# Differences of the feed-forward weights: GpSimd's subtraction, or a DMA that adds the weight onto the negated mean

## The chip, the cores and the metric

One core of a Trainium2 chip runs the kernel. The metric is the device time of one launch in microseconds (us), over several runs.

## The reference, cut to what matters

Two blocks run one after the other on x of 2 x 512 rows and 1024 columns. The first is attention with a small gated layer (256 wide, 1024 inner); its details do not matter here. The second is a feed-forward layer (1024 wide, 3584 inner) whose three weights are first replaced by a coarse form of themselves:

```
def _binary_diff_weight(w, base):
    d = w - base
    coeff = jnp.mean(jnp.abs(d))
    return base + coeff * jnp.sign(d)
W1, W2, W3 = (_binary_diff_weight(w, mean_w) for the three)
gate = jnp.einsum('bsh,ih->bsi', hidden_states, W1)
up = jnp.einsum('bsh,ih->bsi', hidden_states, W3)
h = jax.nn.silu(gate) * up
return jnp.einsum('bsi,hi->bsh', h, W2)
```

`coeff` is one number for a whole weight of 3584 x 1024, so all of `w - base` must have been summed before the first product with that weight is finished. Each weight and its mean are 14.7 MB.

## The kernel before, in words

All is float32. Every product of the feed-forward layer is made in three passes: each operand is split in an upper part (rounded to the matmul's float32r) and a lower part (what is left).

The inner 3584 is cut in 28 tiles j of 128, so each weight has 28 tiles of 128 x 1024 (512 KB). `NEED` lists the 84 of them in the order of use, numbered n: w1, w3, w1, w3 of two tiles j, then (one group later) w2, w2 of the two tiles before. So n = 0 to 7 are w1 and w3 of tiles 0 to 3, n = 8 and 9 the first two of w2. TensorE spends 48 matmuls of 512 columns on each n (lines 1012 and 1034).

A tile is **prepared** in a chain over four engines, in one of three slots `raws[n % 3]` (a weight buffer `raw_w` and a mean buffer `raw_base`): SyncE (SP, line 796 and 797) loads both as soon as the lower part of tile n - 3, which had the slot, is made; GpSimd subtracts the mean (`difference`, line 1735); ScalarE takes the sign (`sign`, L1230); VectorE makes coeff * sign + mean (`whole_weight`, L1533); ScalarE rounds it (`upper`, L1248); VectorE takes the rest (`lower`, L1542).

A tile is **measured** for its coefficient by a load of its own, a subtraction (GpSimd L1730 or VectorE L1700), and a sum of absolute values (ScalarE, `sum_up`, L1225). 70 of the 84 tiles are measured beside the attention block, in an order that a planner writes out. The last 14, all of w2 (t = 70 to 83), are measured at the start of the feed-forward layer in three buffers `late`: SP loads three of them behind the load of each tile n = 5, 6, 7, 8 and the last two behind n = 9 (`LOADED_AFTER`; load t waits for `sum_up` of t - 3), GpSimd subtracts two behind each of its differences n = 5 to 9 (`DIFFERED_AFTER`), VectorE the other four, and ScalarE sums 1, 2, 3, 3, 3, 2 of them at the end of its steps n = 0 to 5 (`SUMMED_IN`).

Behind the planner's part each engine works through n = 0 to 83 in an order that is fixed in the code. ScalarE at step n: round tile n + 2; if n is a w1, silu of the gate of both batches, each of which waits for its products; the sign of tile n + 3 (between the two silus); then the `sum_up`s. TensorE makes the last sum of the coefficient of w2 itself, between steps n = 6 and 7 (L1123): it waits there for VectorE's `csum` (L1521), and that for all 84 tiles. Tiles n = 0, 1, 2 (`EARLY`) are prepared and their first batch is multiplied in the planner's part.

Of the kernel before, what the change touches and what calls it, by code (L numbers as in the profile page):

```python
# [11 lines left out]
ALU = mybir.AluOpType  # L12
ACT = mybir.ActivationFunctionType
# [152 lines left out]
EARLY = len(EARLY_BANK)  # L166
# [194 lines left out]
def phase_one_order():  # L361
# [66 lines left out]
    while ready:  # L428
# [85 lines left out]
NEED = [(which, g - back + kk) for g in range(0, JT + GROUP, GROUP) for kk, which, back in  # L514
        ((0, "w1", 0), (0, "w3", 0), (1, "w1", 0), (1, "w3", 0), (0, "w2", GROUP), (1, "w2", GROUP)) if 0 <= g - back < JT]
# [1 line left out]

LOADED_AFTER, SUMMED_IN = {5: 3, 6: 3, 7: 3, 8: 3, 9: 2}, {0: 1, 1: 2, 2: 3, 3: 3, 4: 3, 5: 2}
SUMMED, LATE_HERE = 6, {1: 2, 2: 5, 3: 8, 4: 11}
DIFFERED_AFTER = {5: 2, 6: 2, 7: 2, 8: 2, 9: 2}  # L520
RAWS, W13, W2 = 3, 3, 3


def bass_layer(nc: bass.Bass, d: dict, out: bass.AP):
    with ExitStack() as whole:
        def sem(name):
            return whole.enter_context(nc.semaphore(name))

        def sems(names):
            return [sem(n) for n in names.split()]  # L530
# [141 lines left out]
        bk_v, fi_v, fi_q, fi_x, fi_var, fi_pow, fi_ok = sems("bk_v fi_v fi_q fi_x fi_var fi_pow fi_ok")  # L672
        me_dve, me_pool, me_abs, c_ones, c_sum, c_mm, c_ok = sems("me_dve me_pool me_abs c_ones c_sum c_mm c_ok")
        n_wk, n_t, n_hi, n_lo = sems("n_wk n_t n_hi n_lo")
        f_diff, f_sign, f_w, f_hi, f_lo = sems("f_diff f_sign f_w f_hi f_lo")
        g_mm, g_silu, g_mul, g_hhi, g_hlo, o_mm, o_acc = sems("g_mm g_silu g_mul g_hhi g_hlo o_mm o_acc")

        order, banks_of, had, turned_had, set_of, set_had, had_last = phase_one_order()
# [112 lines left out]
        @block.sync  # L791
        def _(sp):
            def load_raw(n):
                which, j = NEED[n]
                w, base = raws[n % RAWS]
                sp.dma_start(w[:, :], d[which][j]).then_inc(ld_raw[n % RAWS], 16)
                sp.dma_start(base[:, :], d["mean_" + which][j]).then_inc(ld_raw[n % RAWS], 16)

            sp.dma_start(ident[:, :], d["ident"]).then_inc(ld_const, 16)
            sp.dma_start(cmask, d["cmask"]).then_inc(ld_const, 16)  # L800
            sp.dma_start(pos_i[:, :], d["pos"]).then_inc(ld_const, 16)
            sp.dma_start(inv[:, :], d["inv_freq"]).then_inc(ld_const, 16)
            sp.dma_start(gb[:, :, :, :], d["gb"]).then_inc(ld_const, 16)
            for t in range(TPB):
                sp.dma_start(x_at(t), d["x"][t]).then_inc(ld_x[t], 16)
                if t == 1:
                    sp.dma_start(w_in[0], d["w_in0"]).then_inc(ld_win0, 16)
                    sp.dma_start(wqkv[:, :, :], d["wqkv"]).then_inc(ld_wqkv, 16)
            sp.dma_start(w_in[1], d["w_in1"]).then_inc(ld_win1, 16)
            for t in (TPB, TPB + 1):  # L810
                sp.dma_start(x_at(t), d["x"][t]).then_inc(ld_x[t], 16)
            for n, ld in enumerate((ld_wr0, ld_wr1)):
                sp.dma_start(wcat[n][:, :, :], d[f"wcat{n}"]).then_inc(ld, 16)
                sp.dma_start(bias_ab[n][:, :], d[f"bias_ab{n}"]).then_inc(ld, 16)
                sp.dma_start(dut[n][:, :], d[f"dut{n}"]).then_inc(ld, 16)
            for engine, stage, t, part in order:
                if engine != "SP":
                    continue
                if stage == "measure":
                    n, j = divmod(t, JT)  # L820
                    if t >= PARTS:
                        sp.wait_ge(me_abs, t - PARTS + 1)
                    if t == LATER:
                        sp.wait_ge(at_pv, TURN[last_unit("T", len(GROUPS) // 2 - 1)] + 1)
                    w, base = measured(t)
                    sp.dma_start(w, d[NAMES[n]][j]).then_inc(ld_part[t % PARTS], 16)
                    sp.dma_start(base, d["mean_" + NAMES[n]][j]).then_inc(ld_part[t % PARTS], 16)
                elif stage == "ctx":
                    sp.wait_ge(me_abs, LATER)
                    sp.dma_start(ctxw[:, :, :, :], d["ctx"]).then_inc(ld_ctx, 16)  # L830
                elif stage == "x":
                    sp.wait_ge(fr_ln, t - 1)
                    sp.dma_start(x_at(t), d["x"][t]).then_inc(ld_x[t], 16)
                elif stage == "finish":
                    sp.wait_ge(fr_wide, TILES)
                    if t:
                        sp.wait_ge(fi_q, t)
                        sp.wait_ge(fi_x, t)
                    sp.dma_start(qk_xa[:, :], d["x"][t]).then_inc(ld_again, 16)
                elif stage == "raw":  # L840
                    attention_over(sp)
                    load_raw(t)
            t = SOON
            for n in range(EARLY, len(NEED)):
                sp.wait_ge(f_lo, n - RAWS + 1)
                load_raw(n)
                for _ in range(LOADED_AFTER.get(n, 0)):
                    if t == SOON:
                        phase_one_over(sp)
                    elif t >= SOON + W2:  # L850
                        sp.wait_ge(me_abs, t - W2 + 1)
                    which, j = divmod(t, JT)
                    w, base = measured(t)
                    sp.dma_start(w, d[NAMES[which]][j]).then_inc(ld_late[(t - SOON) % W2], 16)
                    sp.dma_start(base, d["mean_" + NAMES[which]][j]).then_inc(ld_late[(t - SOON) % W2], 16)
                    t += 1
            for t in range(TILES):
                sp.wait_ge(o_acc, (JT // GROUP - 1) * 2 * TILES + 2 * t + 2)
                sp.dma_start(out[t], works[t % 3][:, :]).then_inc(stored[t % 3], 16)
            for n in range(3):  # L860
                sp.wait_ge(stored[n], 16 * len(range(n, TILES, 3)))
# [267 lines left out]
        def _(act):  # L1129
# [96 lines left out]

            def sign(n):
                w = raws[n % RAWS][0]
                act.wait_ge(f_diff, n + 1)
                act.activation(w[:, :], w[:, :], ACT.Sign).then_inc(f_sign, 1)  # L1230

            def upper(n):
                which, j = NEED[n]
# [96 lines left out]
            def split_upper(j):  # L1330

                for b in range(BATCH):
                    act.wait_ge(g_mul, 2 * j + b + 1)
                    if j >= JT - GROUP:
                        act.wait_ge(g_mm, gate_turn(2 * (JT - GROUP) + 1 + j % GROUP, 1))
                    elif j >= GROUP and b == 0:
                        act.wait_ge(o_mm, 2 * TILES * (j // GROUP))
                    act.activation(split(j)[0][:, b * SEQ:(b + 1) * SEQ], held[j % GROUP][:, b * SEQ:(b + 1) * SEQ], ACT.Copy
                                   ).then_inc(g_hhi, 1)
# [3 lines left out]
            for n, (which, j) in enumerate(NEED):  # L1343
                if n == SUMMED:
                    split_upper(j - GROUP)
                if EARLY <= n + 2 < len(NEED):
                    upper(n + 2)
                if which == "w1" and j >= GROUP and n != SUMMED:
                    split_upper(j - GROUP)
                elif which == "w2" and JT - 2 * GROUP <= j < JT - GROUP:  # L1350
                    split_upper(j + GROUP)
                for b in range(BATCH):
                    if which == "w1":
                        act.wait_ge(g_mm, gate_turn(2 * j, b))
                        if j:
                            act.wait_ge(g_mul, 2 * j - 1 + b)
                        act.activation(sgf[b][:, :], banks[gate_bank(2 * j, b)], ACT.Silu).then_inc(g_silu, 1)  # L1357
                    if b == 0 and n + RAWS < len(NEED):
                        sign(n + RAWS)
                for _ in range(SUMMED_IN.get(n, 0)):  # L1360
                    sum_up(t)
                    t += 1
# [340 lines left out]
        def _(pool):  # L1703
# [27 lines left out]

            def difference(n):
                w, base = raws[n % RAWS]
                pool.wait_ge(ld_raw[n % RAWS], 32 * (n // RAWS + 1))
                pool.tensor_tensor(w[:, :], w[:, :], base[:, :], ALU.subtract).then_inc(f_diff, 1)  # L1735

            pool.memset(power[:, :], -0.5).then_inc(consts, 1)
            pool.wait_ge(consts, 1)
# [40 lines left out]

            t = SOON  # L1780
            for n in range(EARLY, len(NEED)):
                difference(n)
                for _ in range(DIFFERED_AFTER.get(n, 0)):
                    t += measurer(t) == "DVE"
                    pool.wait_ge(ld_late[(t - SOON) % W2], 32 * ((t - SOON) // W2 + 1))
                    measure(t)
                    t += 1
# [75 lines left out]
```

## Time and profile before

| | |
|---|---|
| three runs | 1370.82, 1373.15, 1372.25 us; median 1372.25 us |
| profiled execution, first to last instruction (span) | 1373.3 us |
| TensorE busy | 1281.7 us, 93% |
| VectorE, ScalarE, GpSimd busy | 59%, 38%, 27% |
| mean granted TensorE clock | 0.963 of full speed |
| DMA over the span | 197.55 MB, mean 144 GB/s |

The profiled execution has no other time of its own than its span. The span stands 1.05 us above the median of the runs. PE is TensorE, PEld its weight loads, DVE VectorE, ACT ScalarE, POOL GpSimd, SP SyncE; L1012 is line 1012. In the table of windows the columns are the stretch, its length, then each engine's busy us (and its instructions), the granted clock as a share of full speed, the share of the DMA engines and the GB/s.

### The profile page before, as it was taken

The page shows a single profiled execution, that of the slowest core. Times are in us where ns is not written, and L with a number is a line of the kernel's source. Part 1 is how long each engine was busy: PE and PEld are TensorE (multiplying, and loading weights), DVE is VectorE, ACT ScalarE, POOL GpSimd, SP SyncE. Part 2 cuts the span into 40 slices and gives each one's busy share as a digit, 9 for nine tenths or more (in the row PEclk, how much of TensorE's full clock was granted, in tenths as well). Part 3 has the DMA queues.
Part 4 walks back from the last instruction along what each step waited for, and adds up shares of the span by engine and source line. Part 5 has one row for each costly group of instructions (what it writes and reads, how often), then busy time and mean ns, then how long its engine had stood idle before and what let it go on. Part 6 is the DMA issues. An engine that isn't in the chain of part 4 may idle for free.

```text
span 1373.3 us, 16761 instructions
## 1 busy us (share of the span) xinstructions
PE 1281.7 (93%) x6548; PEld 1009.1 (73%) x6548; DVE 816.9 (59%) x1130; ACT 523.2 (38%) x809; POOL 370.7 (27%) x202
## 2 busy tenths in 40 slices
PE   4988787888889899999999999999999999999998
PEld 3754454556566788888888888888888888888887
DVE  6667677767778666545555554536373736454555
ACT  4776565475756454222222212131222222222220
POOL 2122232243422465222222222222222222222210
PEclk9999897789998999999999999999999999999999
DMA  7466667887210594232222323222222222223202
GB/s 286 160 241 219 229 223 268 311 313 281 109 40 17 199 375 176 94 121 93 92 93 92 103 98 107 92 92 92 92 102 101 105 92 92 93 92 118 95 33 123
DMA packets 53826, 197.55 MB, mean 144 GB/s; under 512 B 6626, under 2 KB 6900, under 8 KB 53236
## 3 DMA queue, kind: packets, MB, share of 16 engines
q1 hardware_dynamic: 53748, 196.49, 39.5%
q8 instruction: 52, 0.85, 0.2%
q14 instruction: 26, 0.21, 0.0%
HBM read 192.27 MB, written 4.19 MB: 143 GB/s over the span
## 4 chain that ended last, share of the span: by engine, by line
PE 80%; DVE 9%; ACT 5%; DMA 2%; issue 2%; POOL 1%; SPq 0%; DVEq 0%; ACTq 0%
PE pair L1012 39%; PE quad L1034 22%; PE pair L995 3%; DVE negwide L1446 2%; PE quad L948 2%; DMA late<-in_mean_w 2%; PE quad L958 2%; PE pair L1087 2%; PE pair L867 1%; PE pair L921 1%; PE pair L886 1%; PE pair L901 1%; POOL late L1730 1%; PE pair L1068 1%; PE quad L951 1%
## 5 line engine op out<-in xcount | busy, mean ns | idle before, releaser
L1735 POOL TENSOR_TENSOR raw_w<-raw_w,raw_base 128x1024 f32<-128x1024 f32 x84 | 213.9, 2547 | 631.1 <-DMA raw_base<-in_mean_w 631.1
L1012 PE MATMUL pair<-xnT_hi,w_hi 128*128 128x512 f32 x880 | 343.0, 390 | 1.0 <-DVE xnT_lo L1637 1.0
L1012 PE MATMUL pair<-xnT_hi,w_lo 128*128 128x512 f32 x880 | 342.5, 389 | 0.0
L1012 PE MATMUL pair<-xnT_lo,w_hi 128*128 128x512 f32 x880 | 342.4, 389 | 0.0
L1248 ACT ACTIVATE w_hi<-raw_w 128x1024 fp32r<-128x1024 f32 x84 | 89.0, 1060 | 491.2 <-DVE raw_w L1533 490.8
L1684 DVE TENSOR_TENSOR work<-sgf,pair 128x512 f32<-128x512 f32 x56 | 38.4, 686 | 281.8 <-PE pair L1012 281.8
L1012 PEld LDWEIGHTS pair<-xnT_hi,w_hi 128*128 128x128 f32 x880 | 165.3, 188 | 35.5 <-DVE xnT_lo L1637 1.4
L1012 PEld LDWEIGHTS pair<-xnT_lo,w_hi 128*128 128x128 f32 x880 | 165.3, 188 | 34.5
L1012 PEld LDWEIGHTS pair<-xnT_hi,w_lo 128*128 128x128 f32 x880 | 165.3, 188 | 34.2
L1651 DVE TENSOR_TENSOR hid<-hid,quad 128x512 f32<-128x512 f32 x208 | 139.2, 682 | 67.0 <-PE quad L1034 67.0
L1034 PE MATMUL quad<-w_hi,h_lo 128*128 128x512 f32 x416 | 161.8, 389 | 0.0
L1034 PE MATMUL quad<-w_hi,h_hi 128*128 128x512 f32 x416 | 161.8, 389 | 0.0
L1034 PE MATMUL quad<-w_lo,h_hi 128*128 128x512 f32 x416 | 161.8, 389 | 0.0
L1542 DVE TENSOR_TENSOR w_lo<-raw_w,w_hi 128x1024 fp32r<-128x1024 f32 x84 | 126.5, 1507 | 35.3 <-ACT w_hi L1248 35.3
L1533 DVE SCALAR_TENSOR_TENSOR raw_w<-raw_w,coeff,raw_base 128x1024 f32<-128x1024 f32 x84 | 136.8, 1630 | 13.3 <-ACT raw_w L1230 13.0
L1034 PEld LDWEIGHTS quad<-w_lo,h_hi 128*128 128x128 f32 x416 | 78.1, 188 | 16.3
L1034 PEld LDWEIGHTS quad<-w_hi,h_hi 128*128 128x128 f32 x416 | 78.1, 188 | 16.2
L1034 PEld LDWEIGHTS quad<-w_hi,h_lo 128*128 128x128 f32 x416 | 78.1, 188 | 16.2
L1230 ACT ACTIVATE raw_w<-raw_w 128x1024 f32<-128x1024 f32 x84 | 88.0, 1048 | 0.6 <-POOL raw_w L1735 0.5
L1357 ACT ACTIVATE sgf<-pair 128x512 f32<-128x512 f32 x54 | 32.2, 596 | 122.2 <-PE pair L1012 122.2
L1730 POOL TENSOR_TENSOR ctxw<-ctxw 128x1024 f32<-128x1024 f32 x14 | 35.2, 2515 | 94.6 <-DMA ctxw<-in_mean_w 94.6
L1446 DVE TENSOR_REDUCE negwide<-quad 128x4 f32<-128x512 f32 (+3 forms) x32 | 46.9, 1488 | 20.9 <-PE quad L951 20.6
(239 smaller groups left out, 1569.6 us busy)
## 6 DMA issues: line engine op xcount, KB each, us to landing
raw_w<-in_w SPq DMA_DIRECT2D x84, 512.0 KB, 3.7
raw_base<-in_mean_w SPq DMA_DIRECT2D x84, 512.0 KB, 4.6
ctxw<-in_w SPq DMA_DIRECT2D x28, 512.0 KB, 4.2
ctxw<-in_mean_w SPq DMA_DIRECT2D x28, 512.0 KB, 5.3
part<-in_w SPq DMA_DIRECT2D x24, 512.0 KB, 4.0
part<-in_mean_w SPq DMA_DIRECT2D x24, 512.0 KB, 5.2
big<-in_w SPq DMA_DIRECT2D x18, 512.0 KB, 3.9
big<-in_mean_w SPq DMA_DIRECT2D x18, 512.0 KB, 5.5
```

Source lines behind the costliest of these rows:

```text
L995: a = pe.matmul(bank[:, 0:NZ], lhs, wcat[n][:, k, :], start=k == 0, stop=k == kt - 1)
L1012: a = pe.matmul(banks[gate_bank(u, b)], ww[:, k, :], xx[:, k, :], start=k == 0 and n == 0, stop=k == KF - 1 and n == 2)
L1034: a = pe.matmul(banks[m % 4], hh[:, t * P:(t + 1) * P], ww[:, half * BANK:(half + 1) * BANK], start=kk == 0 and n == 0, stop=kk == GROUP - ...
L1230: act.activation(w[:, :], w[:, :], ACT.Sign).then_inc(f_sign, 1)
L1248: act.activation(hi, raws[n % RAWS][0][:, :], ACT.Copy).then_inc(f_hi, 1)
L1446: a = dve.tensor_reduce(found.rearrange("p r j -> p (r j)"), quad[:, :, at:at + cols], AX.X, ALU.max, negate=True)
L1533: dve.scalar_tensor_tensor(w[:, :], w[:, :], coeff[:, k:k + 1], base[:, :], ALU.mult, ALU.add).then_inc(f_w, 1)
L1542: dve.tensor_tensor(lo, raws[n % RAWS][0][:, :], hi.bitcast(F32), ALU.subtract).then_inc(f_lo, 1)
L1651: dve.tensor_tensor(target, rows, banks[m % 4].rearrange("p (c k j) -> p c k j", c=2, j=32), ALU.add).then_inc(o_acc, 1)
L1684: dve.tensor_tensor(held[j % GROUP][:, b * SEQ:(b + 1) * SEQ], sgf[b][:, :], banks[gate_bank(u, b)], ALU.mult).then_inc(g_mul, 1)
L1730: pool.tensor_tensor(w, w, base, ALU.subtract).then_inc(me_pool, 1)
L1735: pool.tensor_tensor(w[:, :], w[:, :], base[:, :], ALU.subtract).then_inc(f_diff, 1)
```

## The change

From tile n = 3 on GpSimd no longer subtracts. SP loads only the mean; ScalarE writes the negated mean into `raw_w` (`negative`), at the head of its step n - 3; GpSimd then issues a DMA that adds the weight from memory onto it (`added`); ScalarE takes the sign when that DMA has landed. The sign moves behind both silus of its step. GpSimd's ten late measurements move two tiles ahead in its queue.

```
-DIFFERED_AFTER = {5: 2, 6: 2, 7: 2, 8: 2, 9: 2}
+DIFFERED_AFTER = {3: 2, 4: 2, 5: 2, 6: 2, 7: 2}
...
@@ SP, load_raw
-                sp.dma_start(w[:, :], d[which][j]).then_inc(ld_raw[n % RAWS], 16)
+                if n < EARLY:
+                    sp.dma_start(w[:, :], d[which][j]).then_inc(ld_raw[n % RAWS], 16)
                 sp.dma_start(base[:, :], d["mean_" + which][j]).then_inc(ld_raw[n % RAWS], 16)
...
@@ ScalarE
             def sign(n):
                 w = raws[n % RAWS][0]
-                act.wait_ge(f_diff, n + 1)
+                if n < EARLY:
+                    act.wait_ge(f_diff, n + 1)
+                else:
+                    act.wait_ge(ld_add[n % RAWS], 16 * (n // RAWS))
                 act.activation(w[:, :], w[:, :], ACT.Sign).then_inc(f_sign, 1)
+
+            def negative(n):
+                w, base = raws[n % RAWS]
+                act.wait_ge(ld_raw[n % RAWS], 32 + 16 * (n // RAWS))
+                act.activation(w[:, :], base[:, :], ACT.Copy, scale=-1.0).then_inc(f_neg, 1)
...
                 if n == SUMMED:
                     split_upper(j - GROUP)
+                if n + RAWS < len(NEED):
+                    negative(n + RAWS)
                 if EARLY <= n + 2 < len(NEED):
                     upper(n + 2)
...
-                    if b == 0 and n + RAWS < len(NEED):
-                        sign(n + RAWS)
+                if n + RAWS < len(NEED):
+                    sign(n + RAWS)
                 for _ in range(SUMMED_IN.get(n, 0)):
                     sum_up(t)
...
@@ GpSimd
+            def added(n):
+                which, j = NEED[n]
+                pool.wait_ge(f_neg, n - EARLY + 1)
+                pool.dma_start(raws[n % RAWS][0][:, :], d[which][j], accum_op=ALU.add).then_inc(ld_add[n % RAWS], 16)
...
             t = SOON
             for n in range(EARLY, len(NEED)):
-                difference(n)
+                added(n)
                 for _ in range(DIFFERED_AFTER.get(n, 0)):
```

## Rows read from the trace of the kernel before

**Rows 1.** The page's part 2: the span in 40 slices.

```profile
PE   4988787888889899999999999999999999999998
PEclk9999897789998999999999999999999999999999
DMA  7466667887210594232222323222222222223202
```

**Rows 2.** The table of windows over the feed-forward layer.

```profile
470.00:531.00 61.00, 60.14 (x264) 49.47 (x264) 35.53 (x26) 32.55 (x50) 37.78 (x15) 1.00 0.78 296
564.00:1326.00 762.00, 762.00 (x3363) 630.97 (x3362) 389.17 (x413) 190.98 (x236) 179.76 (x70) 1.00 0.27 96
```

**Rows 3.** The chain that ended last: start us, us, what.

```profile
461.27 2.34 DVE x_stat L1383
463.64 1.24 ACT work L1259
...
470.64 5.75 PE pair L1012 x24
...
503.03 1.16 ACT late L1225 x2
504.21 0.33 SPq L854
...
504.58 6.00 DMA late<-in_mean_w
...
510.65 2.76 POOL late L1730
513.43 1.16 ACT late L1225 x2
...
528.25 0.53 ACT h_hi L1338
...
531.19 0.38 PE quad L1123 x2
...
542.59 21.76 PE quad L1034 x96
```

**Rows 4.** VectorE, order of time; the last bracket is idle time before, and its releaser.

```profile
460.53 0.15 DVE L1383 SCALAR_TENSOR_TENSOR x_stat<-x_stat 128x1 f32<-128x1 f32 x1
```

**Rows 5.** GpSimd, order of time.

```profile
461.21 7.03 POOL L1735 TENSOR_TENSOR raw_w<-raw_w,raw_base 128x1024 f32<-128x1024 f32 x3
```

**Rows 6.** ScalarE, order of time.

```profile
460.71 1.25 ACT L1259 ACTIVATE work<-hid,x_stat 128x1024 f32<-128x1024 f32 x1 [10.15 <-DVE x_stat L1383]
468.30 1.03 ACT L1268 ACTIVATE xnT_hi<-quad 128x1024 fp32r<-128x1024 f32 x1 [2.50 <-PE quad L867]
476.41 0.60 ACT L1357 ACTIVATE sgf<-pair 128x512 f32<-128x512 f32 x1 [4.23 <-PE pair L1012]
478.89 1.05 ACT L1230 ACTIVATE raw_w<-raw_w 128x1024 f32<-128x1024 f32 x1
```

**Rows 7.** Issue to landing, one line each of the tiles raw_w, raw_base and late.

```profile
DMA to landing us min/median/max: 3.5/3.7/7.6
DMA to landing us min/median/max: 4.4/4.6/5.9
DMA to landing us min/median/max: 3.7/6.3/9.4
```

**Rows 8.** The table of windows, where the late loads run.

```profile
482.00:522.00 40.00, 40.00 (x179) 33.10 (x177) 27.18 (x18) 22.47 (x34) 26.73 (x11) 1.00 1.01 385
```

**Rows 9.** TensorE alone in single microseconds, about its last pause before the layer.

```profile
437.00:438.00 1.00, 0.20 (x1) 1.00 0.00 0
439.00:440.00 1.00, 1.00 (x3) 0.50 0.00 0
447.00:448.00 1.00, 1.00 (x8) 0.50 0.83 303
449.00:450.00 1.00, 1.00 (x6) 1.00 1.04 406
```

More of the change, by code:

```diff
@@ L674, in bass_layer @@
         n_wk, n_t, n_hi, n_lo = sems("n_wk n_t n_hi n_lo")
-        f_diff, f_sign, f_w, f_hi, f_lo = sems("f_diff f_sign f_w f_hi f_lo")
+        f_diff, f_neg, f_sign, f_w, f_hi, f_lo = sems("f_diff f_neg f_sign f_w f_hi f_lo")
+        ld_add = [sem(f"ld_add{n}") for n in range(RAWS)]
         g_mm, g_silu, g_mul, g_hhi, g_hlo, o_mm, o_acc = sems("g_mm g_silu g_mul g_hhi g_hlo o_mm o_acc")
@@ L1733, in difference @@
                 w, base = raws[n % RAWS]
-                pool.wait_ge(ld_raw[n % RAWS], 32 * (n // RAWS + 1))
+                pool.wait_ge(ld_raw[n % RAWS], 32)
                 pool.tensor_tensor(w[:, :], w[:, :], base[:, :], ALU.subtract).then_inc(f_diff, 1)
+            def added(n):
+                which, j = NEED[n]
+                pool.wait_ge(f_neg, n - EARLY + 1)
+                pool.dma_start(raws[n % RAWS][0][:, :], d[which][j], accum_op=ALU.add).then_inc(ld_add[n % RAWS], 16)
             pool.memset(power[:, :], -0.5).then_inc(consts, 1)
```

## The prediction

> **What bounds the kernel now.** I read the 40 slices first [rows 1]. From slice 16 on TensorE stands at 9 or more and its clock at full speed, so whatever the feed-forward layer does for the weights is hidden behind matmuls there. The table of windows makes it sharp: from 564 to 1326 us TensorE is busy in all 762.00 us, while GpSimd has 179.76 and ScalarE 190.98, and the DMA engines a share of 0.27 [rows 2]. The chain of waits has the beat: 21.76 us for two tiles of w2, so 10.88 us a tile n [rows 3]. Nothing can be won in this stretch; it can only be lost, if a tile's preparation comes to need over 10.88 us on one engine in a row.
>
> The other stretch is 461 to 531 us. There the last measurements of w2 run, and the chain that ended last goes through them and not through TensorE: sum_up, SP's issue, 6.00 us of a late load, 2.76 us of GpSimd, sum_up again, once in 10.4 us (503.03 to 513.43), until L1123 at 531.19 us [rows 3]. TensorE arrives there at the same time: it is busy in 60.14 of the 61.00 us from 470 to 531 [rows 2]. So two chains are balanced, and each us that the measurements lose is a us of TensorE's pause at L1123 and of the end. The DMA engines are full from 482 to 522 us, share 1.01 at 385 GB/s [rows 8].
>
> **Removed: 81 subtractions of GpSimd.** In the stretch at full TensorE they cost nothing, and give nothing back. The first three do cost: they start at 461.21 us and take 7.03 us [rows 5], and VectorE's one-column operation L1383, 0.15 us a moment earlier [rows 4], takes 2.34 us from 461.27, exactly until the first subtraction is over [rows 3]. ScalarE, free at 461.96 [rows 6], waits for it until 463.64 [rows 3]. With GpSimd only waiting, norm, transposes and splits of the last row tile follow 1.68 us earlier, and TensorE's stream starts at 468.96 and not 470.64. The most that this can give is 1.68, and the 0.4 us for which TensorE waits at L1123: 2.1 us, if the measurements follow.
>
> **Moved: the chain of a sign.** After the change ScalarE itself holds a round trip in its own queue: negate n + 3, GpSimd's DMA, sign of n + 3, and only then its `sum_up`s. Call L the time from the end of the negation to the landing of the accumulate. The trace has no such DMA. From below: the fastest plain 512 KB load lands 3.5 us after its issue, the median 3.7. From above: the slowest late load took 9.4 us, their median 6.3 in the crowded stretch where the first accumulates will run too [rows 7]. I take L = 6.0, near that median: the stretch will be less crowded, but the DMA has to read its destination too and GpSimd has to issue it. The Trainium skill, Collectives: The Full Stack, section "Why ReduceScatter is half of AllGather", has an add inside a DMA read two sources and so move at half the rate of a copy. At the 385 GB/s of rows 8 a second 512 KB is 1.36 us, so by that rule an undisturbed L would be some 5.1 us, an estimate, and the sum below 4.5 us less; no run here shows it yet.
>
> What queues behind the waiting sign(4), sign(5), ... on ScalarE are the sums, and for the sums wait SP's late loads (load t for the sum of t - 3), for these GpSimd's measurements, and behind those in GpSimd's queue stands the next `added`. With the new order of GpSimd (two measurements behind each of tiles 3 to 7) this is one closed ring, in which nothing overlaps. Its parts: a sum 1.1 us (1.16 for the sum with its read-out, [rows 3]); SP and the landing 5.5 us (0.33 for the issue and 6.00 in the row of the full queue [rows 3], 4.6 for the landing when it is not full [rows 7]; I take the middle); a measurement 2.4 us (three subtractions in 7.03 us, [rows 5]); L 6.0; a sign or a negation 1.0 us [rows 6].
>
> - Start. Negation of tile 3 behind the last norm of ScalarE, which began at 468.30 and now 1.7 us earlier [rows 6]: done at 468.6, landed at 474.6. The second silu of step 0 was at 476.41 [rows 6], now 474.7; sign(3) therefore ends at 476.2, the sum of t = 70 at 477.3, negation(4) at 478.3, its DMA lands at 484.3 and sign(4) ends at 485.3. Before, it ran at 478.89 [rows 6], so 5.4 us are lost already.
> - sign(4) to sign(5): sum of 71, load of 74, its measurement, added(5), sign(5): 1.1 + 5.5 + 2.4 + 6.0 + 1.0 = 16.0 us, to 501.3.
> - sign(5) to sign(8), three rounds in which both measurements wait for loads freed behind the sign: 1.1 + 5.5 + 4.8 + 6.0 + 1.0 = 18.4 us each against 10.4 before, to 556.5.
> - The last two sums 2.2 us, then split and csum as before (528.25 to 531.19, 3.0 us, [rows 3]): L1123 at 561.7 us in place of 531.2. **That is 30.5 us.**
>
> On the way tile 6 comes late as well: sign(6) ends at 519.7, is rounded only in step 4 behind negation(7), so some 6 us after TensorE wants it at about 518. This costs nothing beyond, since TensorE then still waits over 20 us at L1123.
>
> **TensorE's clock.** After such a pause it does not resume at full speed. The only like place: it hardly worked from 437 us, the granted clock was 0.50 (1.2 GHz) by 439 and still at 447, and full at 449 [rows 9]. Some 9.8 us at the half level cost at most 4.9 us; nothing if the clock holds. I take 3.5.
>
> **Behind L1123.** The outputs need tile 9 at 561.7 + 0.4 + 10.9 = 573.0. ScalarE: from 558.7 split 1.1, negation 1.0, L 6.0, sign 1.0, then three operations on as many elements as the sign's, at most some 1.2 each: 571.4. It fits by 1.6 us; from L = 7.6 each us costs once more.
>
> **The 75 tiles afterwards.** In a row on ScalarE stand negation, L and sign: 8.0 us of 10.88, with the rounding inside the wait. The negation adds 70 us to 190.98 of 762, still only a third busy; the second read adds at most half to a DMA share of 0.27. Free, covered by TensorE's full 762 us, up to L = 8.9.
>
> **Sum.** 30.5 + 3.5 = 34 us on the profiled span of 1373.3 us, which gives 1407.3; the median of the runs stands 1.05 us under the span and is what I predict from: 1372.25 + 34 = 1406 us. The ring has L five times (tiles 4 to 8), so L = 3.5 gives 1394, L = 7.5 gives 1414, L = 8.9 some 1422.
>
> **Rivals.**
> - Slow accumulate. L over 8.9 makes ScalarE's row longer than a tile of TensorE. At 9.4, the slowest landing in the trace: 17 for the ring, 1.8 for tile 9, (11.4 - 10.88) x 75 = 39 for the stream: 1406 + 58 = 1464 us, and 75 us more for each further us. For: a new kind of DMA with a second read. Against: 9.4 was seen only in a full queue; from 564 us on the share is 0.27.
> - Bandwidth alone. ScalarE reaches its signs after the landings, and only the second reads of five accumulates count where the queue is full: 5 x 1.36 = 6.8 us, 1379 us. For: share 1.01 [rows 8]. Against: the ring as laid out leaves the queue idle between its parts. It decides if L plus the wait for `added` stays under what ScalarE has to do anyway. The Trainium skill, DMA: Bandwidth & Descriptors, "Issuing engines are not separate DMA queues", says that GpSimd's DMAs share the 16 engines with SP's; rows here cannot show it.
> - Not slower. The same, but the measurements are carried by the loads that are 2.2 us earlier (SP waits for the operation delayed at 461.27) and by GpSimd free of its subtractions; then only the earlier start is left, 1372.25 - 2.1 = 1370 us. It decides if every `added` is issued before the measurements that now stand ahead of it have to wait for a load. In the order of the code they do wait.
>
> **How the numbers follow.** Ring as worked out, 0.72 (own range 1388 to 1425: L from 3.5 to 8.9, with a few us for the crowding and the clock); slow accumulate 0.13; bandwidth 0.08; not slower 0.07. The range 1378 to 1445 leaves out the last and most of the second. This kernel's measurement can tell 0.2%, 2.7 us, from no change. Slower 0.92; within 0.2%: 0.06; faster 0.02, since more than 2.1 us is nowhere to be had.
>
> **What would show it.** After: L1383 at 461.27 in 0.15 us and the stream from about 469 (start right); sum_ups of the late tiles in groups 18 us apart, each behind a sign that waited for a DMA (ring right); L read as negation's end to sign's start; L1123 near 562, a pause of TensorE over 20 us ahead of it, a few us of half clock behind; from 600 to 1330 us TensorE busy throughout. Wrong, if the groups stay 10 to 11 us apart, or if TensorE has pauses after 600 us.

## The result and the profile after

The kernel after takes 1404.64 us (median of 4 runs, 1402.0 to 1408.04), beside 1372.7 us for the kernel before (4 runs, 1370.82 to 1379.4). The ratio is 1.0225, 95% interval 1.0191 to 1.0259: slower by 26 to 36 us. Forecast were 1406 us. (The 1372.25 us that the prediction starts from are the first three of the four runs of the kernel before.) The profiled execution took 1402.0 us; its span is 1400.2 us.

The page after, slices first (tenths of 35 us each). The line of TensorE answers to [rows 1] and differs most in the slices from 490 to 560 us (the first counted as 0: 14 and 15), where two 9s have become a 7 and a 4, and the clock shows a 6. The DMA line carries 3 to 5 from slice 16 on, where it had mostly 2 and 3. The last two rows are from parts 3 and 6, the added DMA as a queue (packets, MB, share of 16 engines' time) and as an issue (KB, us to landing).

```profile
PE   4888777888988974999999999999999999999998
PEclk9998897898999996999999999999999999999999
DMA  7565666886211765534345343444443534434432
...
q0 software_dynamic: 11664, 42.47, 18.3%
...
raw_w<-in_w POOLq DMA_DIRECT2D x81, 512.0 KB, 5.4
```

The table of windows of the kernel after (busy us and instructions of TensorE, its weight loads, VectorE, ScalarE, GpSimd; granted clock; DMA share; GB/s). The first three rows are the start-up of the feed-forward layer, the last the stream that answers to the second row of [rows 2]:

```profile
470.00:520.00 50.00, 43.18 (x190) 35.14 (x188) 14.79 (x14) 21.17 (x33) 12.53 (x7) 0.99 0.66 202
520.00:540.00 20.00, 12.69 (x48) 10.05 (x48) 8.64 (x7) 8.96 (x14) 5.73 (x3) 0.84 0.75 245
540.00:560.00 20.00, 3.92 (x10) 3.24 (x11) 4.41 (x8) 6.90 (x11) 6.37 (x4) 0.50 0.43 107
600.00:1350.00 750.00, 750.00 (x3311) 621.23 (x3309) 342.27 (x407) 259.82 (x300) 60.41 (x69) 1.00 0.43 96
```

TensorE works in all 750.00 us of the stream, as before. The loss is all ahead of 565 us. The chain that ended last (start us, us, what) shows it; it answers to [rows 3]:

```profile
463.67 5.75 PE pair L1014 x24
...
472.02 0.96 ACT raw_w L1240
472.98 0.30 issue
473.28 5.39 DMA raw_w<-in_w
478.67 0.02 issue
478.69 0.03 ACT raw_w L1235
...
497.02 2.18 ACT late L1227 x4
499.21 0.02 issue
499.22 0.33 SPq L856
499.55 0.04 issue
499.59 7.46 DMA late<-in_mean_w
507.05 0.07 issue
507.12 2.34 POOL late L1742
509.46 5.34 DMA raw_w<-in_w
514.80 0.02 issue
514.83 0.04 ACT raw_w L1235
...
556.08 0.58 PE quad L1125 x2
556.66 12.86 PE pair L1014 x48
```

Read it as a ring: two sums, SP's issue, the landing of a late load, a measurement on GpSimd, the accumulate, the sign, and then sums again. A round takes 18.8 us here: 496.06 to 514.83. In the kernel before a round of the chain had no sign and no raw load in it. The 10.4 us of [rows 3] are the shortest of its rounds: from the issue of one late load in its chain to that of the next it took 11.2, 11.9 and 10.4 us, and in the kernel after 18.4, 18.8 and 18.1 us (issues at 480.81, 499.22, 517.99 and 536.12). These three rounds are 21.8 us of the loss; 6.7 lie ahead of the first of these loads and 3.4 behind the last. The issues in the chain of the kernel before, beside the one at 504.21 of [rows 3]:

```profile
481.12 0.43 SPq L854
...
492.35 0.33 SPq L854
...
514.60 0.33 SPq L854
```

The program up to the norm is the same, but one execution can reach the same instruction up to 9 us earlier than another: VectorE's last TENSOR_SCALAR ahead of the norm begins between 454.8 and 463.9 us in the twelve traces here. So I count from the start of TensorE's stream, and from the statistics to it:

| stretch, us | before | after | difference |
|---|---|---|---|
| VectorE's last TENSOR_SCALAR on x_stat (L1379, after L1391) to stream (460.46 to 470.64; 454.82 to 463.67) | 10.18 | 8.85 | -1.3 |
| stream to the coefficient's matmuls (L1123 at 531.19; L1125 at 556.08) | 60.55 | 92.41 | +31.9 |
| the 48 matmuls behind them | 11.01 | 12.86 | +1.85 |
| from their end to TensorE's last matmul (542.59 to 1369.48; 569.52 to 1396.41) | 826.9 | 826.9 | 0 |

The sum is +32.4, inside the 26 to 36 us of the ratio. The coefficient's two matmuls themselves, between the second and the third row, took 0.2 us more.

### The profile page after: what moved, and what is told of

It reads as the page before. It is cut to its first block, busy times and chain, and to the rows that moved or that the text cites. A ratio compares the mean times of both kernels' runs of the same rounds, so it can differ in the third digit from the quotient of the medians.

```text
span 1400.2 us, 16761 instructions
## 1 busy us (share of the span) xinstructions
PE 1280.8 (91%) x6548; PEld 1011.8 (72%) x6548; DVE 766.5 (55%) x1130; ACT 607.0 (43%) x890; POOL 231.8 (17%) x202
## 3 DMA queue, kind: packets, MB, share of 16 engines
q0 software_dynamic: 11664, 42.47, 18.3%
## 4 chain that ended last, share of the span: by engine, by line
PE 78%; DVE 8%; ACT 5%; DMA 5%; issue 2%; POOL 1%; SPq 0%; DVEq 0%; ACTq 0%
PE pair L1014 39%; PE quad L1036 22%; DVE negwide L1458 2%; DMA late<-in_mean_w 2%; PE quad L960 2%; DMA raw_w<-in_w 2%; PE quad L950 2%; PE pair L997 2%; PE pair L869 1%; PE pair L1089 1%; PE pair L888 1%; PE pair L903 1%; ACT prob L1179 1%; DMA part<-in_mean_w 1%; PE pair L923 1%
## 5 line engine op out<-in xcount | busy, mean ns | idle before, releaser
L1014 PE MATMUL pair<-xnT_hi,w_hi 128*128 128x512 f32 x880 | 345.0, 392 | 10.8 <-ACT sgf L1369 7.8
L1545 DVE SCALAR_TENSOR_TENSOR raw_w<-raw_w,coeff,raw_base 128x1024 f32<-128x1024 f32 x84 | 107.5, 1281 | 197.2 <-ACT raw_w L1235 197.1
L1752 POOL DMA_DIRECT2D raw_w<-in_w x81 | 71.1, 878 | 753.1 <-ACT raw_w L1240 745.5
L1663 DVE TENSOR_TENSOR hid<-hid,quad 128x512 f32<-128x512 f32 x208 | 142.5, 686 | 81.3 <-PE quad L1036 81.3
L1554 DVE TENSOR_TENSOR w_lo<-raw_w,w_hi 128x1024 fp32r<-128x1024 f32 x84 | 102.6, 1222 | 42.3 <-ACT w_hi L1258 42.3
L1240 ACT ACTIVATE raw_w<-raw_base 128x1024 f32<-128x1024 f32 x81 | 84.6, 1045 | 0.0
```

Of the source, the lines that this page charges most:

```text
L1014: a = pe.matmul(banks[gate_bank(u, b)], ww[:, k, :], xx[:, k, :], start=k == 0 and n == 0, stop=k == KF - 1 and n == 2)
L1240: act.activation(w[:, :], base[:, :], ACT.Copy, scale=-1.0).then_inc(f_neg, 1)
L1545: dve.scalar_tensor_tensor(w[:, :], w[:, :], coeff[:, k:k + 1], base[:, :], ALU.mult, ALU.add).then_inc(f_w, 1)
L1554: dve.tensor_tensor(lo, raws[n % RAWS][0][:, :], hi.bitcast(F32), ALU.subtract).then_inc(f_lo, 1)
L1663: dve.tensor_tensor(target, rows, banks[m % 4].rearrange("p (c k j) -> p c k j", c=2, j=32), ALU.add).then_inc(o_acc, 1)
L1752: pool.dma_start(raws[n % RAWS][0][:, :], d[which][j], accum_op=ALU.add).then_inc(ld_add[n % RAWS], 16)
```

## The experiments

Times of a run with one execution are given beside one execution or the median of the kernel before from the same chip; such a time is good to a few us, so these runs are read by stretches of their traces. "Stream to coefficient" is 60.55 in the kernel before and 92.41 in the one after.

**Only the stream.** Tiles 3 to 9 keep the subtraction, the accumulates run from tile 10 on, and `DIFFERED_AFTER` is the old one.

```
+ADDED = 10
...
-                if n < EARLY:
+                if n < ADDED:
...
+                    if b == 0 and n + RAWS < ADDED:
+                        sign(n + RAWS)
+                if ADDED <= n + RAWS < len(NEED):
                     sign(n + RAWS)
...
-                added(n)
+                (difference if n < ADDED else added)(n)
```

> Accumulating DMAs only from tile n = 10 on; tiles 3 to 9 are loaded, subtracted and signed as in the kernel before, with GpSimd's old order of late measurements. Theory (the ring of the late measurements is the whole price, the 74 other accumulates are free): the time of the kernel before within 0.2%, 60.5 us from the start of TensorE's stream to the coefficient's matmul, TensorE busy throughout behind it. Rival (the accumulates also cost in the stream, by ScalarE's longer row, by their second read or by half clock): over half of the 31 us stays, so 1388 us or more.

Measured: 1373.52 us, ratio 0.9991 (0.9966 to 1.0016). Stream to coefficient 60.14. Its window in the stream:

```profile
600.00:1320.00 720.00, 720.00 (x3178) 596.20 (x3177) 332.37 (x398) 248.00 (x286) 57.78 (x66) 1.00 0.43 97
```

The queue of the accumulates in the same stretch (packets, MB, share of 16 engines' time):

```profile
q0 software_dynamic: 9560, 34.84, 29.0%
```

The 74 accumulates of the stream cost nothing that can be measured. All of the loss belongs to the accumulates of tiles 3 to 9 and to GpSimd's new order of measurements, which this run takes back together with them. The two can't be taken apart this way: with the old order and an accumulate for tile 5, the sum of t = 70 in ScalarE's step 0 would wait for a measurement behind `added(5)`, and that for the negation of step 2.

**Sums ahead of the sign.** The kernel after with two lines of ScalarE exchanged, nothing else:

```
-                if n + RAWS < len(NEED):
-                    sign(n + RAWS)
                 for _ in range(SUMMED_IN.get(n, 0)):
                     sum_up(t)
                     t += 1
+                if n + RAWS < len(NEED):
+                    sign(n + RAWS)
```

> The changed kernel with one thing moved: in each step of ScalarE the sums of the late tiles stand ahead of the sign that waits for the accumulate. Same DMAs, same bytes. Theory (ring of negation, accumulate, sign, sum, load, measurement, through ScalarE's and GpSimd's queues): the landing and the sign leave the ring, a round falls from 18.3 to some 12 to 13 us, the coefficient's matmul comes 73 us behind the start of the stream in place of 92.4, time about 1384 us. Rival (bandwidth: the second reads of the accumulates fill the queue): nothing changes, 92 us and 1404 us.

Measured: 1386.39 us, ratio 1.0104 (1.0064 to 1.0144). Stream to coefficient 539.08 - 465.55 = 73.5. The signs of tiles 4 to 8 start 18.1, 9.8, 17.5 and 10.0 us apart, 13.8 in the mean, where 12 to 13 were expected. So 18.9 of the 31.9 us lay in the order alone: sums that had all they needed stood behind a sign that waited for a DMA. What is left of the ring closes through the load of the mean (SP's queue has it ahead of the late loads). Its chain:

```profile
502.29 2.24 DVE w_lo L1554
504.53 0.02 issue
504.55 0.33 SPq L799
...
506.79 9.68 DMA late<-in_mean_w
516.47 0.07 issue
516.53 2.46 POOL late L1742
```

**A copy in place of the accumulate.** The same DMA without the addition; the values are then not the reference's differences.

```
-                pool.dma_start(raws[n % RAWS][0][:, :], d[which][j], accum_op=ALU.add).then_inc(ld_add[n % RAWS], 16)
+                pool.dma_start(raws[n % RAWS][0][:, :], d[which][j]).then_inc(ld_add[n % RAWS], 16)
```

> The changed kernel with GpSimd's DMA as a plain copy over the negated mean, so the addition is left out. Splits the landing time into what the second read costs and what GpSimd's issue costs. Theory (the ring has the landing five times): if the copy lands in 4.0 us and not 5.4, the coefficient's matmul comes 5 x 1.4 = 7 us sooner, 85 us behind the start of the stream, time about 1396 us, and the copy takes about half the DMA engines' time of the accumulate. Rival (the addition costs nothing, GpSimd's software queue is what is slow): landing stays at 5.4 us, 92 us, 1404 us.

Measured: 1394.75 us in one execution, the kernel before 1374.38 there. Stream to coefficient 548.18 - 465.88 = 82.3, so 10.1 us less than with the accumulate; the chain has one such DMA per round, five in all:

```profile
490.30 3.48 DMA raw_w<-in_w
...
506.79 3.57 DMA raw_w<-in_w
...
523.27 3.42 DMA raw_w<-in_w
...
539.41 3.62 DMA raw_w<-in_w
```

The fifth, ahead of these, took 3.50 us. With the addition they took 5.39, 5.49, 5.34, 5.21 and 5.39 us: 1.85 us more each and 9.2 in all. The q0 row of 600 to 1320 us gives the rest: the same bytes as in the kernel with accumulates (29.0%, above) at half of the engines' time.

```profile
q0 software_dynamic: 9584, 34.87, 14.9%
```

**The start alone.** The kernel before, in which GpSimd holds its first subtraction back until its part of the norm is done:

```
             t = SOON
+            pool.wait_ge(fi_ok, TILES)
             for n in range(EARLY, len(NEED)):
                 difference(n)
```

> The kernel before with one wait more: GpSimd's first difference in its part behind the planner's (tile 3) waits until the statistics of all 8 row tiles are done. Theory (this subtraction holds VectorE's one-column operation for 2.2 us at the end of the first block): that operation takes 0.15 us in place of 2.33, TensorE's stream starts 1.7 us sooner measured from the statistics, and as the late loads start sooner too the time falls by about 1.7 us, to 1371 us or less than this measurement can tell. Rival: the operation stays long for another reason, no change.

Measured: 1374.51 us, ratio 0.9993 (0.9976 to 1.0009). VectorE in this kernel, in order of time:

```profile
462.94 0.15 DVE L1379 TENSOR_SCALAR x_stat<-x_stat 128x1 f32<-128x1 f32 x1
...
463.75 0.16 DVE L1383 SCALAR_TENSOR_TENSOR x_stat<-x_stat 128x1 f32<-128x1 f32 x1 [0.59 <-POOL x_stat L1726]
```

L1383 takes 0.16 us where it took 2.34 beside a running subtraction [rows 3], and the way from L1379 to the stream is 471.50 - 462.94 = 8.56 in place of 10.18: 1.6 us less. The same holds in every trace: this operation takes 2.32 to 2.34 us in the five in which GpSimd subtracts there, and 0.16 in the seven in which it doesn't. In the whole kernel's time the 1.6 us are below what 10 runs tell.

**Measurements spread out.** The kernel after with one measurement behind tile 4 and one behind tile 8:

```
-DIFFERED_AFTER = {3: 2, 4: 2, 5: 2, 6: 2, 7: 2}
+DIFFERED_AFTER = {3: 2, 4: 1, 5: 2, 6: 2, 7: 2, 8: 1}
```

> The changed kernel with GpSimd's second late measurement of each pair behind the next accumulate in its queue and not ahead of it (the first pair stays). Theory (ring): a sign waits for an accumulate that stands behind one measurement only, so each of four rounds loses a measurement, 2.4 us, or a little less; the coefficient's matmul comes some 84 us behind the start of the stream in place of 92.4, time about 1396 us. Rival (ScalarE's queue alone makes the ring, GpSimd's order does not matter): 92 us and 1404 us.

Measured: 1402.98 us in one execution. Stream to coefficient 556.88 - 468.66 = 88.2, between what the theories gave (84 and 92). The chain shows what ate into the gain:

```profile
524.72 2.34 POOL late L1742
527.05 7.72 DMA raw_w<-in_w
...
541.98 2.30 POOL late L1742
544.28 7.45 DMA raw_w<-in_w
```

The four accumulates of the ring (tiles 5 to 8) land in 6.9 to 8.5 us instead of 5.4. SP now issues the mean's load 2.1 to 2.4 us ahead of them, where it was 5.2 to 6.0 us in the kernel after. GpSimd's work behind them is hardly what holds them up: the accumulate of tile 3 in the kernel after has two measurements right behind it and lands in 5.7 us. One round of the chain here goes through TensorE's 48 matmuls (from 507.31 us) and not through a late load.

**Both edits together** (sums ahead of the sign, measurements spread out).

> Sums ahead of the sign and one measurement ahead of each accumulate together. Theory: what is left is the loads, as the ring is open: 70 us from the start of the stream to the coefficient's matmul (73.5 with the sums first alone), time about 1382 us, still 10 us above the kernel before, since an accumulate still stands in GpSimd's and ScalarE's order between two measurements. Rival (the two cures are of the same part and do not add): 73.5 us.

Measured: 1386.34 us in one execution; stream to coefficient 540.58 - 472.54 = 68.0. The DMA engines are full again from 485 to 525 us (share 1.01), and the accumulates and late loads of the chain land in 5.2 to 8.0 us. The whole time is no shorter than with the sums alone (1386.39 us): this execution's stream began 7.0 us later (472.54 against 465.55), so the 5.5 us less are read from the stretch of one trace each, and from nothing else.

**Both edits, and a copy in place of the accumulate** (the addition left out).

> Sums first and one measurement ahead of each DMA, as in the run that has both, but the DMA is a plain copy over the negated mean (the addition is left out). That run still needs 68.0 us from the start of the stream to the coefficient's matmul, 8 more than the kernel before, and the DMA engines are full (share 1.01) from 485 to 525 us at 341 GB/s. Theory (what is left is bandwidth, the second read of the accumulates): 61 us, time within 0.4% of the kernel before. Rival (what is left is the order of the queues): 66 us or more.

Measured: 1377.23 us in one execution, the kernel before 1380.72 in one there. Stream to coefficient 531.79 - 467.66 = 64.1, between the two theories: neither number was hit. From 485 to 525 us the share of the DMA engines is 0.92, and the landings in the crowd are still long:

```profile
489.88 6.30 DMA raw_w<-in_w
...
502.81 7.79 DMA late<-in_mean_w
```

**How much slack the stream has.** The kernel of the first experiment (accumulates from tile 10) with 2, 4 and 3 fills of an unused tile on GpSimd ahead of each accumulate, 0.99 us a fill; this lengthens the row negation, L, sign on ScalarE and little else.

```
                 pool.wait_ge(f_neg, n - ADDED + 1)
+                for k in range(FILLS):
+                    pool.memset(spare[:, :], 0.0).then_inc(filled, 1)
+                    pool.wait_ge(filled, (n - ADDED) * FILLS + k + 1)
                 pool.dma_start(raws[n % RAWS][0][:, :], d[which][j], accum_op=ALU.add).then_inc(ld_add[n % RAWS], 16)
```

> Accumulates from tile n = 10 on only, and GpSimd fills an unused 128 x 1024 tile twice (some 1 us each) ahead of each, so that negation to landing grows from 5.7 to about 7.7 us. Theory (in the stream ScalarE's row of negation, landing, sign, 1.9 us + L, is hidden up to 10.88 us): 9.6 us is under it, TensorE stays busy throughout, time of the kernel before within 0.3%. Rival (each us of L costs some of the stream): TensorE idle between tiles.

> The same with four fills, L about 9.7 us. Theory (row of 1.9 + 9.7 = 11.6 us against 10.88): the stream goes at ScalarE's pace, 0.7 us a tile over 74 tiles, so some 40 to 55 us longer than the kernel before, about 1420 us, with a tile every 11.6 us. Rival (the row is overlapped some other way, the bound is the slot of three tiles, 32.6 us): no change.

> Three fills ahead of each accumulate from tile 10 on. A fill takes 1.0 us, a hop 0.3 us on either side, landing 5.4: L = 9.0 us, ScalarE's row 1.9 + 9.0 = 10.9 us, just at TensorE's 10.88. Theory (threshold at 10.88): a tile every 10.9 to 11.0 us, 0 to 8 us above the kernel before, where four fills cost 85. Rival (cost grows from two fills on in step with L): some 40 us.

Measured, one execution each: 1371.06 us with 2 fills, 1459.67 with 4 and 1470.66 with 3. TensorE's windows with 2 and with 4 fills:

```profile
564.00:1320.00 756.00, 756.00 (x3337) 625.99 (x3336) 344.74 (x410) 262.63 (x303) 193.45 (x209) 1.00 0.43 97
```

```profile
700.00:1300.00 600.00, 562.02 (x2394) 459.21 (x2393) 250.20 (x302) 187.79 (x217) 234.67 (x250) 0.97 0.40 87
```

With 2 fills the row is 2 us longer than in the kernel after and TensorE works all the time: free. With 4 and with 3 fills TensorE waits. The signs of tiles 13 to 83 (from first to last start us) with 4 and with 3 fills:

```profile
L1243 ACT ACTIVATE raw_w<-raw_w x71: 1056/1061/1063, 579.1 to 1421.7; 128x1024 f32<-128x1024 f32 x71
```

```profile
L1243 ACT ACTIVATE raw_w<-raw_w x71: 1056/1060/1063, 579.2 to 1434.3; 128x1024 f32<-128x1024 f32 x71
```

With 4 fills that is a sign every 12.04 us in the mean, one row of ScalarE (three in a row stand at 808.54, 820.37 and 832.07 us), and (12.04 - 10.88) x 74 = 86 us. From the stream's start to TensorE's last matmul the trace has 987.0 us against 898.8 in the kernel before, 88 more, and the run took 85 more than the kernel before there. I had expected 40 to 55, from 11.6 us a tile. The lower clock (0.97) is no part of this: the chain that ended last goes from 540 to 1400 us through no matmul (accumulates 47%, fills 32%, issue 12%, ScalarE 9%), so the slower matmuls lie beside ScalarE's row. With 3 fills a sign comes every 12.22 us, (12.22 - 10.88) x 74 = 99 us, and the trace has 997.1 us, 98 more; the run took 90 more than the kernel before there (1380.72). I had expected at most 8. GpSimd, with 4 fills and then with 3 (start us, us, what):

```profile
814.90 0.87 POOL L1765 DMA_DIRECT2D raw_w<-in_w  x1 [0.30 <-POOL spare L1763]
```

```profile
817.83 0.88 POOL L1765 DMA_DIRECT2D raw_w<-in_w  x1 [0.30 <-POOL spare L1763]
```

SP issues the mean's load of 512 KB at 813.30 in the first, 1.6 us ahead of the accumulate, and at 817.23 in the second, 0.6 us ahead. With 4 fills the accumulates land in 5.5 us (median), with 3 in 6.9. So the row with 3 fills is sign 0.97, negation 1.0, 0.1, fills 3.0, 0.3 and 6.9 = 12.2 us, which is the distance of its signs (812.47, 824.70), and longer than with 4 fills. With 5.4 for the landing it would be 10.8, just free. The kernel after shows the same inside one run: of its accumulates from 565 us on, 11 have a mean's load issued 0.8 us behind them and land in 6.1 to 8.3 us, while the other 62, all further from such a load, land in 5.1 to 6.3 (median 5.4). Why the kernel with 3 fills stays in this phase, and that it would be free in another one, was not tried by itself.

## Why the prediction was right, step by step

- **The stream is free, up to L = 8.9.** Right. 750.00 of 750.00 us busy, the 826.9 us unchanged, the first experiment at 0.9991. L measured: the negation ends at 472.98, the accumulate lands at 478.67, 5.7 us (forecast 6.0). The runs with fills lie on both sides of the 8.9: a median L of 7.8 us (2 fills) is free, 9.8 (4 fills) and 10.2 (3 fills) are not. The longest L is not the one with the most delay added, since the landing itself got longer with 3 fills. One size was off: the second read was to add at most half to the DMA share of 0.27, and the share is 0.43.
- **The start gives 1.68 us.** Right: 1.62 with the subtractions held back, 1.3 in the kernel after, where TensorE came to the transposes only at 456.89 us. The trace alone had it all (one row of 0.15 beside one of 2.34 [rows 3, 4]).
- **The ring.** Right in kind and in length. Signs of tiles 4 to 8 end 17.4, 18.8, 18.1 and 18.0 us apart, where 16.0 and three times 18.4 were forecast; sign(8) starts at 550.95, and the coefficient comes 92.41 us after the stream's start where 92.7 were forecast. Tile 6 was late as foreseen: TensorE paused for 7.8 us (forecast some 6) until 523.04 us, when tile 6 was split (522.15) and the silu behind it in ScalarE's queue was done. ScalarE in order of time, a sign behind the DMA it waited for:

```profile
496.06 1.06 ACT L1235 ACTIVATE raw_w<-raw_w 128x1024 f32<-128x1024 f32 x1 [11.37 <-DMA raw_w<-in_w]
...
514.83 1.06 ACT L1235 ACTIVATE raw_w<-raw_w 128x1024 f32<-128x1024 f32 x1 [12.69 <-DMA raw_w<-in_w]
...
532.95 1.06 ACT L1235 ACTIVATE raw_w<-raw_w 128x1024 f32<-128x1024 f32 x1 [10.06 <-DMA raw_w<-in_w]
```

- **The ring's terms** were less right than their sum. I put both measurements of a round in series, 4.8 us, with a late load of 5.5. In the trace the loads are issued three pairs at a time (498.18, 499.22 and 500.26 us), so they crowd each other: the second lands in 6.7 to 7.5 us, the first measurement is done before that, and GpSimd waits again for 0.74 to 1.49 us. One measurement is in the row, 2.34, and two sums, 2.18: 2.18 + 0.37 + 7.1 + 2.34 + 5.4 + 0.96 = 18.3. The errors (one measurement less, -2.5; a sum more, +1.1; SP's issue and the landing, +2.0; L, -0.6) cancel, and that they cancel is luck, as is that start and ring together (-1.3 + 31.9) come out at the 30.5 us forecast. The comparison with the kernel before was off too: 18.4 stood against 10.4, its shortest round.
- **L five times.** Right: 5 accumulates are in the chain, and their 1.85 us over a copy are 9.2 of the 10.1 us that the copy gave back.
- **Behind L1123.** Right: tile 9's lower part was done at 566.65 us and TensorE took it up at 569.52 without a pause, 2.9 us of room where 1.6 were forecast. The 1.2 us for each of the three operations had no row behind them: the page before has 1.63, 1.06 and 1.51, the page after 1.28, 1.06 and 1.22.
- **TensorE's clock.** Sized too high. A pause of 20.4 us ahead of L1125 took the granted clock to 0.50 (1.2 GHz) from 540 to 560 us, and it is at 1.00 again from 561 us on. The 48 matmuls behind the coefficient took 12.86 us instead of 11.01, and the coefficient's own two took 0.58 instead of 0.38: 2.0 and not 3.5, which is what the whole forecast had too much. The half level had lasted 9.8 us in the place I took the term from [rows 9], here only some 4 us of it lay beside work on the path.
- **The rivals.** Slow accumulate: no accumulate in the kernel after took over 8.3 us from its issue, and their median is 5.4. Bandwidth alone: the second reads are 9.2 us of the ring and not 31.9. With the same DMAs and the same bytes the sums ahead of the sign gave 18.9 us back, and the share from 470 to 520 was 0.66. Not slower: the measurements did wait for loads that were freed behind a sign, in every round.
- **The rule of the Trainium skill.** By the Trainium skill, Collectives: The Full Stack, "Why ReduceScatter is half of AllGather", an add inside a DMA moves at half the rate of a copy. The trace agrees: 29.0% of the engines' time for the bytes for which a copy takes 14.9%. The 5.1 us that I worked out for an undisturbed L fell short of the 5.7 measured, since a landing got 1.85 us longer, not 1.36, and GpSimd's hop of 0.30 comes on top.

The 31.9 us by experiments, each step against the one ahead: 92.4 (after), 73.5 with the sums ahead of the sign, 68.0 with the measurements spread out too, 64.1 with a copy as well, 60.5 (before). So the order of ScalarE's queue is 18.9, GpSimd's order 5.5, the addition 3.9 (10.1 while the ring is closed), and 3.6 stay with the negation, the DMA's round trip and the crowd, not taken apart. The steps' shares depend on the order in which they are taken: spreading alone gave 4.2. Each is read from one trace, so those of a few us are less sure than the 18.9, which the times of four runs bear out (1404.64 to 1386.39 us). No version here is measurably faster than the kernel before.

## What to carry to other kernels

A DMA put in place of an operation takes its whole time from issue to landing into the row of whichever engine waits for it, and everything behind that wait in the engine's queue. In a stream where each tile has 10.88 us and the row is 7.6 (2.0 us of ScalarE and 5.7 of L), this is free; in a start-up ring, where each of its parts waits for the last, it is paid once a round, so look for closed rings first and put work that is ready (here the sums) ahead of the wait. Slack left in a row is no safe margin either: a landing time holds for the loads that happen to run beside it.

## What the runs showed of the hardware

- An accumulating DMA of 512 KB into SBUF lands 5.4 us after its issue (5.1 at least), a copy by the same queue 3.8 in the same stretch; it takes twice the DMA engines' time (29.0% against 14.9%); the instruction on GpSimd takes 0.88 us, without the addition 0.54.
- A landing in company: 5.4 us in the median with no other load issued within 1 us of it, 6.9 with a mean's load 0 to 0.6 us ahead, 6.1 to 8.3 with one 0.8 us behind, up to 8.5 while late loads run.
- VectorE's one-column SCALAR_TENSOR_TENSOR takes 0.16 us, and 2.34 beside GpSimd's subtraction of 128x1024; the subtraction gone, VectorE's large operations also fell, in the page's rows from a mean of 1630 to 1281 ns (xcount 84, with the coefficient) and from 1507 to 1222 ns (w_lo). That gave no time, since VectorE bounds nothing there.
